# Centred weights in place of row means, a sum column in the message products, and looser block borders in a four-layer graph network kernel

## The reference, cut to what matters

```python
def _layernorm(x, axis=-1, eps=1e-05):
    m = jnp.mean(x, axis=axis, keepdims=True)
    v = jnp.var(x, axis=axis, keepdims=True)
    return (x - m) / jnp.sqrt(v + eps)

x = _layernorm(x + L0(x))   # two GCN convolutions: sums of neighbours' rows, products with 96x96 weights
x = _layernorm(x + L1(x))   # two SAGE convolutions
x = _layernorm(x + L2(x))   # [x, sum of edge_weight * x[src]] @ mlp_w.T + mlp_b
x = _layernorm(x + L3(x))
# L3: message = batchnorm(relu([x[row], x[col], batchnorm(relu(edge_attr @ W_edge + b_edge))] @ W_msg + b_msg))
#     result  = segment_sum(message, col) + batchnorm(relu(x @ W_node + b_node))
# batchnorm: column mean and variance over all edges (or nodes), times gamma, plus beta
```

## Time and profile before

| What | Value |
| --- | --- |
| profiled execution | 3312.36 us |
| its span, first to last instruction | 3310.6 us |
| TensorE, busy share of the span | 87% |
| VectorE (DVE) | 55% |
| ScalarE (ACT) | 35% |
| GpSimd (POOL) | 66% |
| mean granted TensorE clock | 0.924 of full |

### The profile page before, as it was taken

How to read it: one execution, slowest core, us unless ns; L and a number is a source line. 1 busy time by engine, 2 the same in 40 slices (tenths; PEclk the granted TensorE clock), 3 DMA queues, 4 the chain that set the end, 5 groups by cost and what they waited for, 6 DMA issues and landing times. The chain is left out here.

```text
span 3310.6 us, 64055 instructions
## 1 busy us (share of the span) xinstructions
PE 2872.6 (87%) x23797; PEld 2524.5 (76%) x23797; DVE 1810.9 (55%) x5600; ACT 1150.1 (35%) x1919; POOL 2189.0 (66%) x2179
## 2 busy tenths in 40 slices
PE   1699999999999999996999999967888878788785
PEld 0377777787788878875999999967878778777775
DVE  6899997233433343438777777565433333333334
ACT  2655555000200010104666666543422222222223
POOL 4466652777477756756777777527777777777772
PEclk9799999999999999997999999978988888888886
DMA  7355555787777877773222222122222222222222
GB/s 164 125 186 181 194 194 194 265 283 271 259 240 258 280 260 241 264 236 72 48 47 47 48 48 51 37 68 70 54 53 46 53 53 46 53 46 53 53 45 51
DMA packets 163984, 433.30 MB, mean 131 GB/s; under 512 B 63603, under 2 KB 105513, under 8 KB 143580
## 3 DMA queue, kind: packets, MB, share of 16 engines
q1 hardware_dynamic: 93998, 304.72, 25.8%
q0 software_dynamic: 69680, 124.50, 17.1%
HBM read 335.49 MB, written 93.53 MB: 130 GB/s over the span
## 5 line engine op out<-in xcount | busy, mean ns | idle before, releaser
L829 POOL DMA_INDIRECT work_all<-parts_dram,idx_all x768 | 826.7, 1076 | 347.7 <-issue 227.6
L1414 PE MATMUL ps<-arena 128*128 128x288 bf16 x7154 | 1026.3, 289 | 1.4 <-DMA arena<-blocks_dram 1.4
L2030 POOL DMA_INDIRECT arena<-table,idx_all x696 | 662.7, 952 | 291.1 <-issue 210.3
L1414 PEld LDWEIGHTS ps<-arena 128*128 128x128 bf16 x7154 | 712.6, 100 | 177.4 <-DVE arena L1026 1.6
L2332 PE MATMUL ps<-M,arena 128*128 128x96 f32 x1664 | 420.8, 352 | 177.6 <-DVE arena L2215 174.4
L1587 POOL DMA_INDIRECT arena<-table,idx_all x400 | 393.4, 983 | 121.9 <-issue 120.7
L2332 PEld LDWEIGHTS ps<-M,arena 128*128 128x128 f32 x1664 | 320.0, 239 | 199.9 <-issue 198.5
L1839 PE MATMUL ps<-arena,X 128*96 128x125 f32 x2156 | 317.0, 272 | 3.1 <-ACT arena L1630 3.1
L1245 PE MATMUL ps<-arena,spare 128*128 128x245 bf16 x975 | 291.8, 306 | 29.9 <-ACT arena L882 17.3
L1831 PE MATMUL ps<-work_all,gathot 128*128 128x245 f32 x1100 | 312.0, 378 | 3.0 <-ACT arena L1630 2.2
L1839 PEld LDWEIGHTS ps<-arena,X 128*96 128x96 f32 x2156 | 278.3, 164 | 26.7 <-ACT arena L1630 4.6
(11 more groups left out here) (407 smaller groups left out, 4587.3 us busy)
## 6 DMA issues: line engine op xcount, KB each, us to landing
arena<-blocks_dram SPq DMA_DIRECT2D x117, 1568.0 KB
blocks_dram<-arena SPq DMA_DIRECT2D x39, 1568.0 KB, 5.8
arena<-table,idx_all POOLq DMA_INDIRECT x1096
parts_dram<-arena SPq DMA_DIRECT2D x28, 504.0 KB, 3.2
work_all<-parts_dram,idx_all POOLq DMA_INDIRECT x768
arena<-eaT_dram SPq DMA_DIRECT2D x10, 624.0 KB, 5.1
eaT_dram<-arena SPq DMA_DIRECT2D x48, 104.0 KB, 2.5
arena<-qtable SPq DMA_DIRECT2D x104, 45.0 KB
```

What stands on the lines that cost most here:

```text
L829: eng.indirect_dma_start(out=gat_rows[kk % 3][:, u, :], out_offset=None, in_=parts_dram[:, :], in_offset=bass.IndirectOffsetOnAxis(ap=idx_ ...
L1414: last = nc.tensor.matmul(apply_ps[n % 2], blk[m % 3][:, b, :], Hs[:, b, :], start=b == 0, stop=b == NB - 1)
L2030: eng.indirect_dma_start(out=rows[g % NROW][:, u, :], out_offset=None, in_=table[:, :], in_offset=bass.IndirectOffsetOnAxis(ap=idx_all[:, ...
```

## The change

- Layers 2 and 3 use weights that are centred beforehand, so that the rows need no mean: in round 3 DVE makes `centring` (identity minus 1/96) and subtracts the row means of `L2WaT` and `L2WbT`; the two transposes that carry the batchnorm scale become products with `centring`.
- The normalisation becomes: add; one square of the whole chunk on ACT; one sum on DVE; root on ACT; reciprocal and one multiply on DVE. Three buffers instead of two; the sum of chunk c and the result of chunk c-1 stand behind the add of chunk c+1.
- In layer 2 the transposes of chunk c+1 go ahead of `source_product(c)`.
- The waits for SP's stores at two block ends move to where the table is used: GpSimd's stream, and DVE's ahead of `target_operands`.
- Layer 2's beginning: three DVE copies and the zero fill of `aggT` move to ACT; TensorE's stray product moves behind six builds.
- Messages: `edge_constants` ahead of the zero fills; the target rows in two buffers, their high part made on ACT.
- The message operands get a column of ones; `sums` are 178 columns wide and `gram_total` holds the total over all messages. The last group is gathered, added and passed through relu in four pairs of tiles.
- Batchnorm has seven chained operations instead of nine. The end drops both reductions over `aggT` and takes three output buffers.

```diff
@@ SP, end of "rounds"
-                eng.wait_ge(stored, 16 * NCH)
@@ DVE, start of round 3
+                    if r == 3:
+                        centre_link(nc.vector.tensor_scalar(centring, ident[0:F, 0:F], -1.0 / F, None, ALU.add))
+                        centre_link(nc.vector.tensor_reduce(row_means, both, AX.X, ALU.add))
+                        centre_link(nc.vector.tensor_scalar(row_means, row_means, -1.0 / F, None, ALU.mult))
+                        centre_link(nc.vector.tensor_tensor(both, both, row_means.unsqueeze(2).to_broadcast([F + 1, 2, F]), ALU.add))
@@ helpers of the normalisation
+        def squares(eng, tt3, sq, root):
+            eng.wait_ge(nd_var, root + 1)
+            nc.scalar.activation(sq, tt3, ACT.Square).then_inc(nd_sq, 1)
+        def stddev(eng, v1, root):
+            eng.wait_ge(nd_red, root + 1)
+            nc.scalar.activation(v1, v1, ACT.Sqrt, bias=eps_col[:, 0:1], scale=1.0 / F).then_inc(nd_sd, 1)
+        def sum_squares(eng, sq, v1, root):
+            eng.wait_ge(nd_sq, root + 1)
+            nc.vector.tensor_reduce(v1, sq, AX.X, ALU.add).then_inc(nd_red, 1)
@@ "layer 2": GpSimd begins with eng.wait_ge(stored, 16 * NCH); SP's last wait (p_tab) goes
@@ ACT, start of "layer 2"
+                nc.scalar.activation(wslo, wslo_h, ACT.Copy).then_inc(w_cols, 1)
+                eng.wait_ge(nd_bias, 1)
+                nc.scalar.activation(wwin[:, 0:4 * NVT], ps6[:, 0:4 * NVT], ACT.Copy).then_inc(w_cols, 1)
+                nc.scalar.activation(wwin[:, 4 * NVT:NTW], ps7[:, 0:NTW - 4 * NVT], ACT.Copy).then_inc(w_cols, 1)
+                nc.scalar.activation(aggT[:, :], zero_col.to_broadcast([F, AW]), ACT.Copy).then_inc(agg_zero, 1)
@@ TensorE, "layer 2"
-                stray_products()
                 for s in range(TOTAL):
+                    if s == WKEYS - 1:
+                        stray_products()
@@ DVE, normalisation of layer 2 (the one of "end" has the same order)
+                first(0)
+                for c in range(NCH):
+                    if c >= 2:
+                        eng.wait_ge(nd_out, c - 1)
+                    if c + 1 < NCH:
+                        first(c + 1)
+                    sum_squares(eng, sqr[c % 2], v1r[c % 2], c)
+                    if c:
+                        second(c - 1)
                 second(NCH - 1)
@@ TensorE, normalisation of layer 2
-                for c in range(NCH):
-                    turn_result(c)
+                for c in range(NCH + 1):
+                    if c < NCH:
+                        turn_result(c)
                     if c + 3 < NCH:
                         result_product(c + 3)
-                    source_product(c)
+                    if c:
+                        source_product(c - 1)
@@ "messages": GpSimd and DVE wait for p_tab
+                eng.wait_ge(p_tab, 16 * NCH)
@@ ACT, preparation
+                def target_high(c):
+                    eng.wait_ge(p_q, c + 2)
+                    eng.wait_ge(m_q[c % 2], c // 2 * 16 + 16)
+                    nc.scalar.activation(qparts[c % 2][:, :, 0, :], qf[c % 2], ACT.Copy).then_inc(p_hi, 1)
@@ TensorE, message sums
-                            last = nc.tensor.matmul(ps[0:F, 0:SUMS], h32[s][:, u, :], operand[s][:, u, :], ...)
+                            last = nc.tensor.matmul(ps[0:F, 0:TOT], h32[s][:, u, :], operand[s][:, u, :], ...)
@@ DVE, last group
+                        if g == NG - 1:
+                            accumulate_sums(g - 1, 1 - r)
+                            add_last_rows(g)
+                            return
@@ "end", DVE
-                link(nc.vector.tensor_reduce(bcol(14), aggT[:, HALF_N:N], AX.X, ALU.add))
-                eng.wait_ge(f_half, 1)
-                link(nc.vector.tensor_tensor(bcol(14), bcol(14), bcol(39), ALU.add))
-                batchnorm(eng, link, bcol(14), msq[:, :], E, "g_msg", "beta_msg", 0, bn_var, bn_sd, 1)
+                batchnorm(eng, link, h_total, msq[:, :], E, "g_msg", "beta_msg", 0, bn_var, bn_sd, 1)
@@ "end", SP: no wait between stores; ahead of the last two, for all earlier ones
+                for i in range(3):
+                    eng.wait_ge(f_dma[i], F_DMA0[i] + 16 * ((NCH - 1 - i + 2) // 3))
```

More of the change, by code:

```diff
@@ L1649, in _ @@
                         edge_sums(EDGE_AT[s])
-                for c in range(NCH + 2):
-                    if c < NCH:
-                        stddev(eng, ttr[c % 2], s1r[c % 2], v1r[c % 2], c)
+                for c in range(-1, NCH + 2):
+                    if c + 1 < NCH:
+                        squares(eng, ttr[(c + 1) % 3], sqr[(c + 1) % 2], c + 1)
+                    if 0 <= c < NCH:
+                        stddev(eng, v1r[c % 2], c)
                     if 1 <= c <= NCH:
@@ L1739, in _ @@
                     keys(t)
-                link(nc.vector.memset(aggT[:, :], 0.0))
-                link.done()
+                eng.wait_ge(agg_zero, 1)
                 stray_sums()
@@ L2107, in messages, with last_messages @@
                         nc.scalar.activation(h32[g % 4], hsum.rearrange("p (u f) -> p u f", f=F), ACT.Relu).then_inc(q["relu"], 1)
+                    def last_messages(g):
+                        for j in range(U // 2):
+                            two = slice(2 * j, 2 * j + 2)
+                            eng.wait_ge(last_hs, k * (U // 2) + (LAST_HS0 + j + 1))
+                            if j == 0:
+                                eng.wait_ge(summed, k * NG + MSG0 + g + 1)
+                            nc.scalar.activation(h32[g % 4][:, two, :], hsum.rearrange("p (u f) -> p u f", f=F)[:, two, :], ACT.Relu).then_inc(last_relu, 1)
+                        eng.wait_ge(last_relu, k * (U // 2) + (LAST_RELU0 + U // 2))
+                        eng.sem_inc(q["relu"], 1)
                     def narrow_hots(g, s):
@@ L2215, in add_rows, with add_last_rows @@
                         nc.vector.tensor_tensor(hsum.rearrange("p (u f) -> p u f", f=F), ps23[:, :, 0:F], rows[g % NROW][:, :, :], ALU.add).then_inc(q["hs"], 1)
+                    def add_last_rows(g):
+                        wait("pre", g)
+                        wait("relu", g - 1)
+                        for j in range(U // 2):
+                            two = slice(2 * j, 2 * j + 2)
+                            eng.wait_ge(last_in[j], k * 32 + (LAST_IN0[j] + 32))
+                            nc.vector.tensor_tensor(hsum.rearrange("p (u f) -> p u f", f=F)[:, two, :], ps23[:, two, 0:F], rows[g % NROW][:, two, :], ALU.add).then_inc(last_hs, 1)
+                        eng.wait_ge(last_hs, k * (U // 2) + (LAST_HS0 + U // 2))
+                        eng.sem_inc(q["hs"], 1)
                     def accumulate_sums(g, r):
@@ L2346, in sums @@
                         r = s % 2
-                        wait("relu", g)
+                        if g < NG - 1:
+                            wait("relu", g)
                         if g - 2 in NODE_AT:
@@ L2388, in _ @@
             def _(eng):
-                nc.scalar.activation(spare[0:F, 0:HALF_N], aggT[:, 0:HALF_N], ACT.Relu, accum_out=bcol(39)).then_inc(f_half, 1)
                 batch_stddev(eng, 0, bn_var, bn_sd, 1)
-                for c in range(NCH):
-                    stddev(eng, ttf[c % 2], s1r[c % 2], v1r[c % 2], c + root0)
+                for c in range(-1, NCH):
+                    if c + 1 < NCH:
+                        squares(eng, ttf[(c + 1) % 3], sqf[(c + 1) % 2], c + 1 + root0)
+                    if c >= 0:
+                        stddev(eng, v1r[c % 2], c + root0)
             @block.vector
```

232 lines of the change are left out of this document (115 added, 117 removed).

## The result

| | before | changed |
| --- | --- | --- |
| median of 12 runs each | 3312.77 us | 3295.52 us |
| lowest to highest | 3303.32 to 3323.23 | 3280.86 to 3302.40 |
| ratio, 95% interval | | 0.9947 (0.9936 to 0.9958) |
| profiled execution, span | 3312.36, 3310.6 | 3280.86, 3279.1 |
| mean granted TensorE clock | 0.924 | 0.924 |

The kernel became 17 us faster, where 25 were forecast (3287); the time lies in the range, though the median stands on the line of 3295 that the prediction drew between faster and not to be told apart. A second series gave 3288.0 against 3307.93, ratio 0.9936 (0.9924 to 0.9948), 20 us. The profiled execution of the changed kernel is its fastest, so its own 31 us are not the median's 17.

A forecast was written before the change was run, and what follows sets the result against it. Message loop bound by GpSimd's issue of gathers, layer 2 by TensorE, with serial stages between; 8.0 + 2.0 + 0.4 + 4.2 + 0.2 + 10.2 = 25.0 us off 3312.4 gave 3287, range 3271 to 3300.

The forecast's parts named there:

- Start and body of layer 2: Layer 2 up to its result products: engines start without SP's store wait, stray sums come earlier; 8.0 us gained, bounds 4 and 9.
- its cap: Layer 2's body: the earlier start can gain at most 8.4 us; beyond that the stage is bound by gathers.
- Rival C: Layer 2: the earlier start doesn't last, gathers land late and only 2 us arrive; 3293 us, chance 0.10.
- Normalisation of layer 2: Layer 2's normalisation: stage falls from 50.4 to 48.4 us with mixed clock levels, 2.0 us gained.
- rival B: Layer 2's normalisation: TensorE at half clock throughout, loss 10.6 us instead of 2.0 gained; about 3299 us, chance 0.12.
- a rise as late as before: Layer 2's normalisation: TensorE's clock falls again and recovers as before, so two rounds take 7.9 us and two 5.75.
- the loop: Layer 2's normalisation: add, result, transposes and products wait on each other in a circle, 5.75 us full clock, 7.9 half.
- A: Rival for layer 2's normalisation: it keeps the full clock and gains 7.4 us; 3281 us in all, chance 0.15.
- Stall ahead of group 6: Start of the message gathers: group 0 is added earlier, so GpSimd's stall goes; 4.2 us gained, bounds 0 and 5.
- rival E: Start of messages: ACT's fill or high parts make ACT late, the stall stays; costs 4 to 8 us, 3293, chance 0.07.
- The end: End block: reductions and two batchnorm operations go, chunks get shorter, last stores wait; 10.2 us gained, bounds 8 and 12.
- Rival D: Message loop: rows of 178 words slow GpSimd's gathers and eat the gain; 3317 us or slower, chance 0.04.

The follow-up runs named there:

- oldstart: Changed kernel with only the start of layer 2 undone (SP's wait, DVE's copies and zero fill, stray products first): 3296.97 us, ratio 0.9968 to the kernel before.
- best3: Changed kernel with TensorE's result product before the transposes, no GpSimd drain at three borders, last stores at once, idle transposes at three places: 3265.87 us, ratio 0.9873.
- after: The changed kernel itself, first series, against the kernel before: 3295.52 us, ratio 0.9947.
- after_again: The changed kernel run once more, nothing altered, against the kernel before: 3288.0 us, ratio 0.9936.
- nodrain: Changed kernel with the three middle block borders made without GpSimd's drain: 3286.95 us, ratio 0.9937 to the kernel before.
- resfirst: Changed kernel with TensorE's result product of chunk c+3 issued ahead of the transposes of chunk c in layer 2's normalisation: 3276.65 us, ratio 0.9892.

## Why the prediction was right or wrong, point by point

**The total.** It lies in the range, and part of that is luck: the normalisation came out 5.0 us worse than forecast, and the other stages together 4.6 us better, so that the stages add to 24.6 us for 25.0 with one of them wrong in sign.

**Start and body of layer 2: 8.0 forecast, 9.3 measured, 7.6 if more profiled executions are taken** (644.7 us for the three with the old start, 637.1 for the six with the new one and the drain). Right, and oldstart shows the cause. One step inside failed: "without SP's wait DVE, ACT and TensorE begin some 0.5 us behind the last engine". They began 4.1 behind it; the wait behind SP's was GpSimd's drain. It cost little, because the shift was near its cap: TensorE took group 58 at 2.05 us behind the last issue, in the 1.7 to 2.5 I had named, in the second execution at 3.24. The cap itself scatters: in the kernel before this distance was 9.64 us in the execution I had read, and 6.4 in the other. Rival C, a start that does not last, is refuted.

**Normalisation of layer 2: 2.0 gained forecast, 3.0 lost.** This is the step that failed, and it is rival B's mechanism with a smaller price. The durations were right: 7.7 us a round for 7.9, 5.53 at full clock for 5.75, the fall after the first wait. What failed is "a rise as late as before": I gave two of the four rounds the half clock, and all four had it. The row that spoke for this, full clock at 2178.30 "although TensorE had waited just before", has a wait of only 0.26 us, too short to carry it. And the reason that I gave for a bound, the loop, was half of it: at 1.2 GHz TensorE's own transposes and two products fill 7.4 us a chunk, which I had not summed. The order therefore looks harmless at half clock and costs 9 us at full (42.6 against 33.3). Rival B, 3299, had put 61 us for the stage, and that was a wrong sum: by the prediction's own terms (8.2, four rounds of 7.9, 5.2 for two more chunks, 9 for the tail) it is 54.0, and B's time 3293. Measured were 53.1 and 53.7. So the mechanism that came is one to which I had given 12%. (The range's lower end, 3271, is no sum of its terms either: A's 3281 with the best start and end gives 3279.) What makes the clock rise late is open.

**Start of the messages: 0.4 forecast, 1.5 measured**, 3.6 us in every execution with the new wait, 5.1 in both of the kernel before. No run separates what made up the other 1.1 us.

**Stall ahead of group 6: 4.2 forecast, 4.6 measured on the gathers' span.** The size is right for a mixed reason: 2.5 us of the stall went (4.47 to 1.99); the rest lies in fewer gathers above 1.1 us and in a second gap, 2.4 us ahead of group 5, that only the second profile of the kernel before has. The first target rows came 9.1 us behind GpSimd's start instead of 6, and the addition of group 0 began 63.0 behind it (67.4 before), when "some 14 us earlier" would be 53. TensorE at half clock was the holder: best3, which adds nothing but idle transposes ahead of and in the preparation, removed the stall. So rival E happened in part.

**Last group: 0.2 forecast**, and in the changed kernel no more can be read: 1.4 us between the means is the scatter of the kernel before (9.7 and 12.1). The changed kernel's 9.5, twice, is GpSimd's drain, which the prediction did not have.

**The end: 10.2 forecast, 10.8 measured.** Batchnorm and reductions 3.9 us for 4.0. Adds 3.0 us apart for 3.05. Chunk 5's store held the last ones by 1.9 us for 1.8: it landed 2.74 us behind its issue. The estimate of 0.9 us that the prediction worked out from the Trainium skill, "DMA: Bandwidth & Descriptors", section "Anatomy of one DMA", left out a part: beside the fixed cost of 2.0 us the section has one for the bytes, at 436 GB/s, and it speaks of DMAs that GpSimd issues. With both parts this store of 336 KB comes to 2.8 us, an estimate by that section, and the 2.74 measured on SP's queue agree with it.

**Inside the loop: nothing forecast, nothing measured.** Rival D, slower gathers, is refuted: one issue each 1.25 us in all executions.

The stages add to 24.6 us without the scatter of the rounds; the two series gave 17 and 20, the upper ends of their intervals 21 and 25. Some 5 us stay open. Part of it may be that the two profiled executions are the fastest of the changed kernel's two series: in the four other kernels with its start and the drain, layer 2's stretch was 1 to 4 us longer than in these two.

## What to carry to other kernels

Before an order of work on TensorE is changed, sum its work per round at both clock levels, and follow the new waits around: a result that stands behind the next add can close a loop over three engines. A short wait of TensorE at the head of a serial stage can cost more in clock than in time; idle matmuls there are cheap to try, and here 1.5 us of them shortened the stage by 2.7 to 10.7 us. Profile a stage more than once before a gain is put down to an edit: the same order took 36.0 and 43.9. A block border waits for every engine, and for GpSimd it waits until its drain is over: look at what stands second behind each wait that you remove.

## What the runs showed of the hardware that I had not expected

- GpSimd's drain ended 8.0 to 9.3 us behind its last indirect gather at the end of the rounds, and 9.21 us behind it at the end of the messages in all nine profiled executions that have it, at a time when the gathered rows had been added. Without it DVE's wait at the border fell by 2.0 and by 1.3 us.
- The granted clock stayed at 1.2 GHz for 37.5, 41.0 and 44.4 us in the normalisation of the changed order (after, after_again, nodrain); in the first of them TensorE was busy for 22.8 of the last 22.9 us. In the order of resfirst it was back after 6.8 or 20.5 us, in the old order after 13.7. The order alone does not decide it: 6.8 and 20.5 belong to the same one. What decides when it rises is open.
- The same code of a stage repeats to 0.01 us when the clock falls and rises at the same places (50.38 in three executions of the old order), and moves when it does not: by 2 us in the changed order (53.1, 53.7, 54.3, 55.2), by 8 in resfirst's. What scatters in this stage is the clock.
